# VectorE's operations inside each step of a 32-step lane chain, in another order

## The chip, the cores and the metric

The kernel runs on one core of a Trainium2 chip. Its time is the device time of one execution in microseconds (us). Three executions of the kernel before took 301.94, 303.7 and 392.66 us, median 303.7. A fourth was profiled: it took 303.54 us, and the span from its first to its last instruction is 301.7 us.

The engines are named as in the profile: PE is TensorE (PEld its weight loads), DVE is VectorE, ACT is ScalarE, POOL is GpSimd, SP is SyncE.

## What is computed

Two blocks of a network on 2048 tokens of width 128, all in fp32. The first block adds to x a recurrent memory and an expert network; the second adds attention and a gated network. The change lies in the recurrent memory alone:

```python
def step(M, kv):
    k_t, v_t = kv
    v_pred = jnp.einsum('bf,bfd->bd', k_t, M)
    surprise = jnp.linalg.norm(v_t - v_pred, axis=-1, keepdims=True)
    delta = k_t[:, :, None] * v_t[:, None, :]
    M = M + eta_c[None, :, None] * surprise[:, :, None] * delta
    return (_ln2(M), None)          # (M - mean) * rsqrt(var + eps), over all of M
M, _ = jax.lax.scan(step, M0, (kT, vT))     # 2048 tokens, one after the other
mem_out = jnp.einsum('btf,bfd->btd', q, M)
```

Only the last M is used. Each step needs one number of the step before, the surprise (a norm), and the spread of M (a variance).

## The kernel before

**The lanes.** The 2048 steps of the recurrence are cut into lanes of L = 32 tokens that overlap by half (HALF = 16), one lane for each of the 128 partitions. So 2048 dependent steps become 32 dependent steps (j = 0 to 31), each on 128 lanes at once. M itself is never formed: a lane keeps the inner products that the norm and the variance need, as short rows of numbers in the tiles ST (running rows), Y (weighted sums of products), Cr and CC (tables). All of them lie in one big tensor, so each reads `arena` in the profile.

**One step of the chain** is written out by hand, and every engine works its instructions off in the order in which they are written. In step j DVE does, by its lines in the kernel before:

- L1375, the scan: one `tensor_tensor_scan` of 17 elements, whose partial sums are what the step needs. It waits for ACT's result g of the step before, and for all that DVE wrote.
- L1382 and L1383, alpha and alpha2: two operations on one element each; the second reads the first. alpha2 releases ACT.
- L1391, the near product: adds a term to Y for the tokens of the same half (210 elements in steps 0 and 16, down to 2 in steps 13 and 29).
- L1397, the far product (steps 0 to 12, `FAR` = 13): 496 down to 304 elements, written to one of three buffers (`N_FP`), for PE, which adds it up in PSUM (L541). In steps 13 to 15 it is instead L1408, straight into Y.
- L1411, the row of squares (1 to 17 elements), and L1413, top (one element): both read Y, so they wait for the product before them.
- L1416, the rows: adds Cr, with the squares in it, to ST. The next scan reads ST.

Step 13 has three more: L1402 (GA), L1405 (GY, which reads what PE summed) and L1406 (a reduction of GY into ST).

**ACT** in step j: L917 (square root of the scan's last sum, after the scan), L919 (a copy), then L922, which waits for alpha2 and for L917 and gives g, the SG entry that scales everything in step j+1. Behind these it does other work in its queue where it falls due: L885 in steps 0 to 2, copies of PE's results (L897, L900 to L903, L907) after steps 5, 6, 7, 9, 10 and 11, and in step 13 the copy L933, for which DVE's L1405 waits. A copy that waits for PE holds up the L917 and L922 queued behind it.

**PE** adds up the far product of each step (L541), and after those of steps 4, 5, 6, 8, 9 and 10 does a piece of another job (L525 to L535), whose result ACT copies. After step 12 it goes on to the expert network (L554) and then has nothing until the chain has ended.

**Waiting inside an engine.** Two helpers order DVE's own work: `did(i)` lets instruction i raise a semaphore when it has finished, and `need(n)` lets the next instruction wait until the nth of these has finished; `last()` is `need` of the newest. An instruction with no such wait may start while the one before it is finishing.

**Behind the chain** come a few small operations, the memory's output (L560), the first block's sum, the second layer norm, and attention with the gated network, to the end.

The change touches the loop over j on DVE, L1360 to L1416.

Of the kernel before, what the change touches and what calls it, by code (L numbers as in the profile page):

```python
# [6 lines left out]
ALU = mybir.AluOpType  # L7
ACT = mybir.ActivationFunctionType
AX = mybir.AxisListType
# [8 lines left out]
HALF = 16  # L18
S = T // HALF
L = 2 * HALF  # L20
W = S
# [20 lines left out]
PAD = 30  # L42
RW = PAD + L + 4
R_G, R_T, R_Q, R_CD, R_D, R_C, R_R, R_B, R_S, R_P, R_E = 0, 1, 2, 5, 6, 9, 10, 13, 14, 15, 16
SCAN = R_E + 1
FAR = 13
FAR_BANK = 4
# [16 lines left out]
class Order:  # L64
# [5 lines left out]
    def did(self, instruction):  # L70
        instruction.then_inc(self.semaphore, 1)
        self.n += 1
        return self.n

    def need(self, n):
        self.engine.wait_ge(self.semaphore, n + self.offset)


def program(nc, a, out):
    with ExitStack() as ctx:  # L80
# [63 lines left out]
        CC = take(3 * (L + 1) * L).rearrange("p (q j t) -> p q j t", q=3, j=L + 1)  # L144
# [4 lines left out]
        Cr = Crf.rearrange("p (j r c) -> p j r c", j=L, r=4)  # L149
# [29 lines left out]
        def near(block, j):  # L179

            n = HALF - 2 - j
            return OJN[block][:, NEAR_AT[j]:NEAR_AT[j] + (n + 1) * n].rearrange("p (l t) -> p l t", t=n)
# [997 lines left out]
        def _(dve):  # L1180
            v = nc.vector
# [4 lines left out]
            def last():  # L1186
                need(o.n)
# [169 lines left out]
            dve.wait_ge(near_ready, 1)  # L1357
            last()

            for j in range(L):  # L1360
                sg = SG[:, j, 1:2]
                n = L - 2 - j
                end = HALF if j < FAR else L

                def of_scan(r):

                    c = PAD + j + 1 + 2 * (r - R_P)
                    return ST[:, R_P, c:c + 1]

                last()  # L1370
                dve.wait_ge(g_ready, j + 1)
                if j == HALF:
                    dve.wait_ge(behind_act, 9)
                c = PAD + j + 1 - 2 * R_P
                v.tensor_tensor_scan(ST[:, R_P, c:c + 2 * SCAN - 1:2], SG[:, j, :], ST[:, :, PAD + j], 0.0, ALU.mult, ALU.add).then_inc(scan_ready, 1)  # L1375
                if j == L - 1:
                    break

                dve.wait_ge(scan_ready, j + 1)
                if j == HALF - 1:  # L1380
                    dve.wait_ge(behind_act, 6)
                need(did(v.scalar_tensor_tensor(out=AL[:, j, 0:1], in0=of_scan(R_R), scalar=of_scan(R_R), in1=of_scan(R_Q), op0=ALU.mult, op1=ALU.add)))  # L1382
                v.scalar_tensor_tensor(out=AL[:, j, 1:2], in0=of_scan(R_E), scalar=VJ[:, j + 1:j + 2], in1=AL[:, j, 0:1], op0=ALU.mult, op1=ALU.add).then_inc(alpha_ready, 1)  # L1383

                jb = j % HALF
                nb = HALF - 2 - jb
                if nb > 0:

                    tail = (j // HALF + 1) * HALF
                    later = Y[:, j:tail - 1, j + 2:tail]  # L1390
                    did(v.scalar_tensor_tensor(out=later, in0=near(j // HALF, jb), scalar=sg, in1=later, op0=ALU.mult, op1=ALU.add))  # L1391
                if j < FAR:

                    if j >= N_FP:
                        dve.wait_ge(far_done, j - N_FP + 1)
                    vc_, a_ = far_factors(j)
                    v.scalar_tensor_tensor(out=FPf[j % N_FP][:, 0:(L - 1 - j) * HALF].rearrange("p (l t) -> p l t", t=HALF), in0=vc_, scalar=sg, in1=a_,  # L1397
                                           op0=ALU.mult, op1=ALU.mult).then_inc(fp_ready, 1)
                elif j < HALF:
                    if j == FAR:  # L1400

                        ga = did(v.tensor_tensor(GA, aT[:, 0:FAR, HALF:L], SG[:, 0:FAR, 1:2].broadcast_to([W, FAR, HALF]), ALU.mult))  # L1402
                        dve.wait_ge(far_act, 1)
                        need(ga)
                        need(did(v.tensor_tensor(GY, GA, PS[:, FAR_BANK, 0:FAR * HALF].rearrange("p (l t) -> p l t", t=HALF), ALU.mult)))  # L1405
                        did(v.tensor_reduce(ST[:, R_Q, PAD + HALF - 1:PAD + L - 1], GY.rearrange("p l t -> p t l"), AX.X, ALU.add))  # L1406
                    later = Y[:, j:L - 1, HALF:L]
                    did(v.scalar_tensor_tensor(out=later, in0=OJF[j - FAR], scalar=sg, in1=later, op0=ALU.mult, op1=ALU.add))  # L1408
                last()
                if end - j - 2 > 0:  # L1410
                    did(v.tensor_tensor(Cr[:, j, 0, j + 1:end - 1], CC[:, 0, j + 1, j + 2:end], Y[:, j, j + 2:end], ALU.mult))  # L1411
                if n > 0:
                    did(v.tensor_tensor(ST[:, R_T, PAD + j + 1:PAD + j + 2], CC[:, 0, j + 2, j + 2:j + 3], Y[:, j + 1, j + 2:j + 3], ALU.mult))  # L1413
                    need(o.n - 1)
                rows = ST[:, R_Q:R_S + 1:4, PAD + j + 1:PAD + L]
                did(v.scalar_tensor_tensor(out=rows, in0=Cr[:, j, :, j + 1:L], scalar=sg, in1=rows, op0=ALU.mult, op1=ALU.add))  # L1416


            dve.wait_ge(h_ready, L)
# [285 lines left out]
```

## Time and profile before

| what | value |
|---|---|
| median of three runs | 303.7 us |
| profiled execution | 303.54 us, its span 301.7 us |
| DVE, PE, ACT busy in the span | 236.7, 246.6, 189.0 us |
| first scan of the chain starts | 52.71 us |
| last scan starts | 106.18 us |
| the chain, from the one to the other | 53.47 us, 31 steps |

A row of a timeline gives an instruction's start and its duration. The distance between the starts of two neighbours is the number to watch in this case: it is sometimes shorter than the duration of the first of them, sometimes longer.

### The profile page before, as it was taken

Reading aid. Unit: us, or ns where it says so; the run is one execution under the profiler, and the core shown is the slowest. Engines: PE = TensorE matmul, PEld = TensorE weight load, DVE = VectorE, ACT = ScalarE, POOL = GpSimd, SP = SyncE. Lnnn points to the kernel's source line nnn. Section 1 sums busy time; section 2 is a strip of 40 time slices with the busy share of each in tenths; the row PEclk is TensorE's granted clock in tenths of the full one; section 3 lists DMA queues with packets and bytes.
Section 4 is the critical chain, followed back from the end, with each engine's and each line's share of the span. In section 5 each row is a group of like instructions: output and inputs, shape, how many; then the busy total and the mean of one; then the engine's idle time right before and its main releaser. Section 6 shows DMA issues by size and latency. Waiting matters only on the chain.

```text
span 301.7 us, 5258 instructions
## 1 busy us (share of the span) xinstructions
PE 246.6 (82%) x1730; PEld 166.5 (55%) x1730; DVE 236.7 (78%) x751; ACT 189.0 (63%) x452; POOL 99.2 (33%) x121
## 2 busy tenths in 40 slices
PE   0599978478830069997999999999998999999991
PEld 0339963133730066564678787777887444444481
DVE  6969789999899848985999997887775566666672
ACT  1249675646344413797787579999963877777630
POOL 8013000000000000789888546998895000000000
PEclk9999999999995555899999999999999999999999
DMA  7600000000000006400300000000000000000013
GB/s 204 184 6 4 2 0 0 3 1 0 0 3 0 1 1 239 180 0 12 130 1 3 0 2 1 0 2 1 2 0 2 0 0 3 0 0 0 3 35 109
DMA packets 8429, 8.57 MB, mean 28 GB/s; under 512 B 1744, under 2 KB 7504, under 8 KB 7888
## 3 DMA queue, kind: packets, MB, share of 16 engines
q1 hardware_dynamic: 7968, 7.91, 8.2%
q10 hardware_dynamic: 432, 0.30, 0.3%
q8 instruction: 16, 0.26, 0.3%
q14 instruction: 13, 0.11, 0.1%
HBM read 7.15 MB, written 1.05 MB: 27 GB/s over the span
## 4 chain that ended last, share of the span: by engine, by line
PE 57%; DVE 30%; ACT 7%; issue 3%; DMA 1%; SPq 0%; DVEq 0%; ACTq 0%
PE PS L749 9%; PE PS L750 9%; PE PS L707 9%; PE PS L687 8%; PE PS L698 4%; PE PS L452 3%; DVE arena L1416 3%; PE PS L467 2%; DVE arena L1382 2%; DVE arena L1397 2%; DVE arena L1383 2%; DVE arena L1375 2%; PE PS L560 2%; DVE arena L1391 2%; PE PS L664 2%
## 5 line engine op out<-in xcount | busy, mean ns | idle before, releaser
L749 PE MATMUL PS<-arena 128*128 128x512 f16 x128 | 48.5, 379 | 0.6 <-issue 0.6
L750 PE MATMUL PS<-arena 128*128 128x512 f16 x128 | 48.5, 379 | 0.0
L1633 DVE TENSOR_TENSOR arena<-arena 128x512 f32<-128x512 f32 x32 | 22.2, 692 | 19.5 <-ACT arena L1082 19.5
L687 PE MATMUL PS<-arena 128*128 128x512 f32 (+3 forms) x80 | 32.0, 531 | 0.4 <-ACT arena L1003 0.4
L1131 POOL CAST arena<-arena 128x512 f16<-128x512 f32 x2 | 1.2, 611 | 90.6 <-DVE x L1501 90.6
L1081 ACT ACTIVATE arena<-PS,arena 128x512 f32<-128x512 f32 x32 | 22.0, 688 | 13.2 <-PE PS L750 13.1
L1123 POOL TENSOR_TENSOR arena<-arena 128x256 f32<-128x256 f32 x32 | 21.6, 675 | 16.0 <-DVE arena L1572 13.7
L1055 ACT ACTIVATE arena<-PS,lnt 128x512 f32<-128x512 f32 (+3 forms) x40 | 25.0, 634 | 1.7 <-DVE lnt L1587 1.6
L1124 POOL TENSOR_TENSOR arena<-arena,small 128x256 f16<-128x256 f32 (+1 forms) x36 | 24.3, 676 | 2.8
L1580 DVE TENSOR_REDUCE mxb<-PS 128x1 f32<-128x512 f32 (+3 forms) x40 | 22.2, 602 | 1.8 <-PE PS L689 1.8
L1082 ACT ACTIVATE arena<-PS,arena 128x512 f16<-128x512 f32 x32 | 21.8, 682 | 0.0
L749 PEld LDWEIGHTS PS<-arena 128*128 128x128 f16 x128 | 12.5, 98 | 15.7 <-issue 0.7
L750 PEld LDWEIGHTS PS<-arena 128*128 128x128 f16 x128 | 12.5, 98 | 15.0
L687 PEld LDWEIGHTS PS<-arena 128*128 128x128 f32 x80 | 14.0, 190 | 12.2 <-issue 10.3
L698 PE MATMUL PS<-con,arena 128*128 128x128 f32 x136 | 19.6, 274 | 0.4 <-ACT arena L1055 0.4
L707 PE MATMUL PS<-arena,xn 128*128 128x128 f32 x144 | 19.3, 279 | 0.4 <-ACT xn L1039 0.2
L917 ACT ACTIVATE arena<-arena 128x1 f32<-128x1 f32 x32 | 6.5, 203 | 20.7 <-DVE arena L1375 20.6
L541 PE MATMUL PS<-arena,con 128*128 128x496 f32 (+12 forms) x26 | 12.2, 551 | 8.8 <-DVE arena L1397 7.3
L707 PEld LDWEIGHTS PS<-arena,xn 128*128 128x128 f32 x144 | 17.4, 191 | 1.5 <-ACT xn L1039 1.1
L568 PE MATMUL PS<-con,arena 128*32 128x1 f32 x2 | 0.3, 202 | 21.4 <-DVE arena L1422 21.4
L707 PE MATMUL PS<-arena 128*128 128x128 f32 x128 | 17.3, 279 | 0.3 <-ACT arena L1039 0.2
L698 PEld LDWEIGHTS PS<-con,arena 128*128 128x128 f32 x136 | 15.1, 141 | 3.6 <-issue 1.7
(263 smaller groups left out, 643.2 us busy)
## 6 DMA issues: line engine op xcount, KB each, us to landing
arena<-h_T SPq DMA_DIRECT2D x2, 1024.0 KB, 4.8
x<-L_attn_x SPq DMA_DIRECT2D x4, 256.0 KB, 4.6
arena<-cos SPq DMA_DIRECT2D x1, 1024.0 KB, 4.7
arena<-sin SPq DMA_DIRECT2D x1, 1024.0 KB, 6.9
out<-arena SPq DMA_DIRECT2D x4, 256.0 KB, 3.3
arena<-w_T SPq DMA_DIRECT2D x3, 256.0 KB, 3.0
con<-shape_constants ACTq DMA_DIRECT2D x1, 192.0 KB, 3.4
w1e<-L_ffn_W SPq DMA_DIRECT2D x1, 128.0 KB, 3.9
```

What stands on the lines that cost most here:

```text
L687: i = mm(PS[:, k, 0:cnt * P], qT1[:, t * P:(t + 1) * P], kT1[:, c * P:(c + cnt) * P], start=True, stop=not last)
L698: i = tr(PS[:, 4 + gi % 2, (b - c) * P:(b - c + 1) * P], Pr[t % 2][:, b * P:(b + 1) * P], ident)
L707: i = mm(PS[:, 7, (t % 4) * D:(t % 4 + 1) * D], PT[t % 2][:, b * P:(b + 1) * P], V1[:, b, :], start=(b == 0), stop=(b == t))
L749: mm(bank(u % 8), wH[:, k, m * P:(m + 1) * P], sH[:, k, cols], start=(k == 0), stop=False)
L750: i = mm(bank(u % 8), wL[:, k, m * P:(m + 1) * P], sL[:, k, cols], start=False, stop=(k == HT4 - 1))
L1055: f(Pr[t % 2][:, c * P:(c + cnt) * P], PS[:, SCORE_BANK[gi], 0:cnt * P], ACT.Exp, scale=1.0 / D, bias=nbs[:, t:t + 1], accum_out=rsums[:, ...
L1081: f(FP[u % 4], bank(u % 8), ACT.Gelu, scale=s_[:, u % HT4:u % HT4 + 1])
L1082: f(high, bank(u % 8), ACT.Gelu, scale=s_[:, u % HT4:u % HT4 + 1]).then_inc(read, 1)
L1123: o.need(o.did(tt(rest, value, high, ALU.subtract)))
L1124: return tt(low, rest, low_scale.broadcast_to([P, cols]), ALU.mult)
L1580: i = did(v.tensor_reduce(mxb[:, gi:gi + 1], PS[:, SCORE_BANK[gi], 0:cnt * P], AX.X, ALU.max))
L1633: v.tensor_tensor(RP[m], FP[m], high, ALU.subtract).then_inc(rest_ready, 1)
```

## The change

Inside each step DVE's operations stand in another order, and each waits for the one operation whose result it needs instead of for the newest. No operation is added or removed (711 instructions of DVE before and after), nothing changes in size, and the queues of the other engines stay as they are.

```diff
--- before.py
+++ after.py
@@ -1357,9 +1357,12 @@
             dve.wait_ge(near_ready, 1)
             last()
 
+            formed = added = o.n
             for j in range(L):
                 sg = SG[:, j, 1:2]
                 n = L - 2 - j
+                jb = j % HALF
+                nb = HALF - 2 - jb
                 end = HALF if j < FAR else L
 
                 def of_scan(r):
@@ -1367,7 +1370,7 @@
                     c = PAD + j + 1 + 2 * (r - R_P)
                     return ST[:, R_P, c:c + 1]
 
-                last()
+                need(max(formed, added))
                 dve.wait_ge(g_ready, j + 1)
                 if j == HALF:
                     dve.wait_ge(behind_act, 9)
@@ -1376,19 +1379,50 @@
                 if j == L - 1:
                     break
 
+                if nb > 0:
+
+                    tail = (j // HALF + 1) * HALF
+                    later = Y[:, j:tail - 1, j + 2:tail]
+                    added = did(v.scalar_tensor_tensor(out=later, in0=near(j // HALF, jb), scalar=sg, in1=later, op0=ALU.mult, op1=ALU.add))
+                if FAR < j < HALF:
+                    later = Y[:, j:L - 1, HALF:L]
+                    added = did(v.scalar_tensor_tensor(out=later, in0=OJF[j - FAR], scalar=sg, in1=later, op0=ALU.mult, op1=ALU.add))
+                if j == FAR:
+
+                    ga = did(v.tensor_tensor(GA, aT[:, 0:FAR, HALF:L], SG[:, 0:FAR, 1:2].broadcast_to([W, FAR, HALF]), ALU.mult))
+
                 dve.wait_ge(scan_ready, j + 1)
+                alpha = did(v.scalar_tensor_tensor(out=AL[:, j, 0:1], in0=of_scan(R_R), scalar=of_scan(R_R), in1=of_scan(R_Q), op0=ALU.mult, op1=ALU.add))
+
+                def row_of_squares():
+
+                    need(added)
+                    return did(v.tensor_tensor(Cr[:, j, 0, j + 1:end - 1], CC[:, 0, j + 1, j + 2:end], Y[:, j, j + 2:end], ALU.mult))
+
+                if end - j - 2 > 0 and j != FAR:
+                    formed = row_of_squares()
+
+                need(alpha)
                 if j == HALF - 1:
                     dve.wait_ge(behind_act, 6)
-                need(did(v.scalar_tensor_tensor(out=AL[:, j, 0:1], in0=of_scan(R_R), scalar=of_scan(R_R), in1=of_scan(R_Q), op0=ALU.mult, op1=ALU.add)))
                 v.scalar_tensor_tensor(out=AL[:, j, 1:2], in0=of_scan(R_E), scalar=VJ[:, j + 1:j + 2], in1=AL[:, j, 0:1], op0=ALU.mult, op1=ALU.add).then_inc(alpha_ready, 1)
 
-                jb = j % HALF
-                nb = HALF - 2 - jb
-                if nb > 0:
-
-                    tail = (j // HALF + 1) * HALF
-                    later = Y[:, j:tail - 1, j + 2:tail]
-                    did(v.scalar_tensor_tensor(out=later, in0=near(j // HALF, jb), scalar=sg, in1=later, op0=ALU.mult, op1=ALU.add))
+                if j == FAR:
+
+                    dve.wait_ge(far_act, 1)
+                    later = Y[:, j:L - 1, HALF:L]
+                    added = did(v.scalar_tensor_tensor(out=later, in0=OJF[j - FAR], scalar=sg, in1=later, op0=ALU.mult, op1=ALU.add))
+                    need(ga)
+                    gy = did(v.tensor_tensor(GY, GA, PS[:, FAR_BANK, 0:FAR * HALF].rearrange("p (l t) -> p l t", t=HALF), ALU.mult))
+                    formed = row_of_squares()
+                    need(gy)
+                    summed = did(v.tensor_reduce(ST[:, R_Q, PAD + HALF - 1:PAD + L - 1], GY.rearrange("p l t -> p t l"), AX.X, ALU.add))
+                if n > 0:
+                    need(added)
+                    top = did(v.tensor_tensor(ST[:, R_T, PAD + j + 1:PAD + j + 2], CC[:, 0, j + 2, j + 2:j + 3], Y[:, j + 1, j + 2:j + 3], ALU.mult))
+                need(summed if j == FAR else formed)
+                rows = ST[:, R_Q:R_S + 1:4, PAD + j + 1:PAD + L]
+                formed = did(v.scalar_tensor_tensor(out=rows, in0=Cr[:, j, :, j + 1:L], scalar=sg, in1=rows, op0=ALU.mult, op1=ALU.add))
                 if j < FAR:
 
                     if j >= N_FP:
@@ -1396,24 +1430,6 @@
                     vc_, a_ = far_factors(j)
                     v.scalar_tensor_tensor(out=FPf[j % N_FP][:, 0:(L - 1 - j) * HALF].rearrange("p (l t) -> p l t", t=HALF), in0=vc_, scalar=sg, in1=a_,
                                            op0=ALU.mult, op1=ALU.mult).then_inc(fp_ready, 1)
-                elif j < HALF:
-                    if j == FAR:
-
-                        ga = did(v.tensor_tensor(GA, aT[:, 0:FAR, HALF:L], SG[:, 0:FAR, 1:2].broadcast_to([W, FAR, HALF]), ALU.mult))
-                        dve.wait_ge(far_act, 1)
-                        need(ga)
-                        need(did(v.tensor_tensor(GY, GA, PS[:, FAR_BANK, 0:FAR * HALF].rearrange("p (l t) -> p l t", t=HALF), ALU.mult)))
-                        did(v.tensor_reduce(ST[:, R_Q, PAD + HALF - 1:PAD + L - 1], GY.rearrange("p l t -> p t l"), AX.X, ALU.add))
-                    later = Y[:, j:L - 1, HALF:L]
-                    did(v.scalar_tensor_tensor(out=later, in0=OJF[j - FAR], scalar=sg, in1=later, op0=ALU.mult, op1=ALU.add))
-                last()
-                if end - j - 2 > 0:
-                    did(v.tensor_tensor(Cr[:, j, 0, j + 1:end - 1], CC[:, 0, j + 1, j + 2:end], Y[:, j, j + 2:end], ALU.mult))
-                if n > 0:
-                    did(v.tensor_tensor(ST[:, R_T, PAD + j + 1:PAD + j + 2], CC[:, 0, j + 2, j + 2:j + 3], Y[:, j + 1, j + 2:j + 3], ALU.mult))
-                    need(o.n - 1)
-                rows = ST[:, R_Q:R_S + 1:4, PAD + j + 1:PAD + L]
-                did(v.scalar_tensor_tensor(out=rows, in0=Cr[:, j, :, j + 1:L], scalar=sg, in1=rows, op0=ALU.mult, op1=ALU.add))
 
 
             dve.wait_ge(h_ready, L)
```

In the order rows below, the line numbers are those of the kernel that is named. The names in all of them are `arena`, so operations are told by line and size; the scan is printed as a SCALAR_TENSOR_TENSOR of 128x17.

DVE, step 4 (a step with a far product; steps 0 to 12 are alike), before: scan, alpha, alpha2, near product, far product, squares, top, rows, next scan.

```order
L1375 SCALAR_TENSOR_TENSOR arena<-arena 128x17 [waits g_ready,dve_order]
L1382 SCALAR_TENSOR_TENSOR arena<-arena 128x1 [waits scan_ready]
L1383 SCALAR_TENSOR_TENSOR arena<-arena 128x1 [waits dve_order]
L1391 SCALAR_TENSOR_TENSOR arena<-arena 128x11x10
L1397 SCALAR_TENSOR_TENSOR arena<-arena 128x432 [waits far_done]
L1411 TENSOR_TENSOR arena<-arena 128x10 [waits dve_order]
L1413 TENSOR_TENSOR arena<-arena 128x1
L1416 SCALAR_TENSOR_TENSOR arena<-arena 128x4x27 [waits dve_order]
L1375 SCALAR_TENSOR_TENSOR arena<-arena 128x17 [waits g_ready,dve_order]
```

The same step in the changed kernel:

```order
L1378 SCALAR_TENSOR_TENSOR arena<-arena 128x17 [waits g_ready,dve_order]
L1386 SCALAR_TENSOR_TENSOR arena<-arena 128x11x10
L1395 SCALAR_TENSOR_TENSOR arena<-arena 128x1 [waits scan_ready]
L1400 TENSOR_TENSOR arena<-arena 128x10 [waits dve_order]
L1408 SCALAR_TENSOR_TENSOR arena<-arena 128x1 [waits dve_order]
L1422 TENSOR_TENSOR arena<-arena 128x1 [waits dve_order]
L1425 SCALAR_TENSOR_TENSOR arena<-arena 128x4x27 [waits dve_order]
L1431 SCALAR_TENSOR_TENSOR arena<-arena 128x432 [waits far_done]
L1378 SCALAR_TENSOR_TENSOR arena<-arena 128x17 [waits g_ready,dve_order]
```

The near product has moved ahead of alpha, the squares between alpha and alpha2, and the far product behind the rows, just ahead of the next scan. Alpha2, which releases ACT, now comes fifth instead of third.

DVE, step 16 (steps 16 to 29 are alike), before:

```order
L1375 SCALAR_TENSOR_TENSOR arena<-arena 128x17 [waits behind_act,g_ready,dve_order]
L1382 SCALAR_TENSOR_TENSOR arena<-arena 128x1 [waits scan_ready]
L1383 SCALAR_TENSOR_TENSOR arena<-arena 128x1 [waits dve_order]
L1391 SCALAR_TENSOR_TENSOR arena<-arena 128x15x14
L1411 TENSOR_TENSOR arena<-arena 128x14 [waits dve_order]
L1413 TENSOR_TENSOR arena<-arena 128x1
L1416 SCALAR_TENSOR_TENSOR arena<-arena 128x4x15 [waits dve_order]
```

And in the changed kernel:

```order
L1378 SCALAR_TENSOR_TENSOR arena<-arena 128x17 [waits behind_act,g_ready,dve_order]
L1386 SCALAR_TENSOR_TENSOR arena<-arena 128x15x14
L1395 SCALAR_TENSOR_TENSOR arena<-arena 128x1 [waits scan_ready]
L1400 TENSOR_TENSOR arena<-arena 128x14 [waits dve_order]
L1408 SCALAR_TENSOR_TENSOR arena<-arena 128x1 [waits dve_order]
L1422 TENSOR_TENSOR arena<-arena 128x1 [waits dve_order]
L1425 SCALAR_TENSOR_TENSOR arena<-arena 128x4x15 [waits dve_order]
```

Here too the near product and the squares now stand ahead of alpha2.

DVE, step 13 in the changed kernel, without its scan. Before, the order was alpha, alpha2, near product, GA, GY (waits for ACT's copy, `far_act`), reduction, far product, squares, top, rows.

```order
L1386 SCALAR_TENSOR_TENSOR arena<-arena 128x2
L1392 TENSOR_TENSOR arena<-arena 128x208
L1395 SCALAR_TENSOR_TENSOR arena<-arena 128x1 [waits scan_ready]
L1408 SCALAR_TENSOR_TENSOR arena<-arena 128x1 [waits dve_order]
L1414 SCALAR_TENSOR_TENSOR arena<-arena 128x18x16 [waits far_act]
L1416 TENSOR_TENSOR arena<-arena,PS 128x208 [waits dve_order]
L1400 TENSOR_TENSOR arena<-arena 128x17 [waits dve_order]
L1419 TENSOR_REDUCE arena<-arena 128x16 [waits dve_order]
L1422 TENSOR_TENSOR arena<-arena 128x1 [waits dve_order]
L1425 SCALAR_TENSOR_TENSOR arena<-arena 128x4x18 [waits dve_order]
```

GA stands ahead of alpha, and the far product (L1414) now also waits for ACT's copy and is the first behind it.

## Rows read from the trace of the kernel before

**Rows 1.** Stretches: length; busy us by engine (instructions), granted PE clock, DMA share, GB/s
```profile
52.70:78.00 25.30, 16.51 (x46) 6.98 (x45) 23.87 (x105) 13.62 (x52) 0.00 (x0) 1.00 0.00 1
...
84.73:106.40 21.67, 1.03 (x10) 0.84 (x8) 19.24 (x103) 10.39 (x45) 0.00 (x0) 0.60 0.00 1
```
**Rows 2.** Waits inside the chain: who waited for whom, us, times, longest
```profile
DVE arena L1375 <- ACT arena L922: 0.4, 1, 0.4
```
**Rows 3.** Timeline of DVE, step 4: start, duration, instruction
```profile
61.27 0.20 DVE L1375 TENSOR_TENSOR_SCAN arena<-arena 128x17 f32<-128x17 f32 x1
61.50 0.22 DVE L1382 SCALAR_TENSOR_TENSOR arena<-arena 128x1 f32<-128x1 f32 x1
61.76 0.22 DVE L1383 SCALAR_TENSOR_TENSOR arena<-arena 128x1 f32<-128x1 f32 x1
61.89 0.33 DVE L1391 SCALAR_TENSOR_TENSOR arena<-arena 128x110 f32<-128x110 f32 x1
62.14 0.66 DVE L1397 SCALAR_TENSOR_TENSOR arena<-arena 128x432 f32<-128x432 f32 x1
62.72 0.16 DVE L1411 TENSOR_TENSOR arena<-arena 128x10 f32<-128x10 f32 x1
62.80 0.15 DVE L1413 TENSOR_TENSOR arena<-arena 128x1 f32<-128x1 f32 x1
62.91 0.33 DVE L1416 SCALAR_TENSOR_TENSOR arena<-arena 128x108 f32<-128x108 f32 x1
63.28 0.19 DVE L1375 TENSOR_TENSOR_SCAN arena<-arena 128x17 f32<-128x17 f32 x1
```
**Rows 4.** Timeline of DVE and ACT, step 30, the last before the last scan
```profile
104.94 0.19 DVE L1375 TENSOR_TENSOR_SCAN arena<-arena 128x17 f32<-128x17 f32 x1
...
105.43 0.22 DVE L1383 SCALAR_TENSOR_TENSOR arena<-arena 128x1 f32<-128x1 f32 x1
...
105.68 0.40 ACT L922 ACTIVATE arena<-arena 128x12 f32<-128x12 f32 x1 [0.21 <-DVE arena L1383]
106.18 0.20 DVE L1375 TENSOR_TENSOR_SCAN arena<-arena 128x17 f32<-128x17 f32 x1 [0.39 <-ACT arena L922]
```
**Rows 5.** Timeline of DVE, step 16, and the start of step 29
```profile
84.73 0.20 DVE L1375 TENSOR_TENSOR_SCAN arena<-arena 128x17 f32<-128x17 f32 x1
...
85.35 0.43 DVE L1391 SCALAR_TENSOR_TENSOR arena<-arena 128x210 f32<-128x210 f32 x1
...
86.34 0.19 DVE L1375 TENSOR_TENSOR_SCAN arena<-arena 128x17 f32<-128x17 f32 x1
...
103.62 0.19 DVE L1375 TENSOR_TENSOR_SCAN arena<-arena 128x17 f32<-128x17 f32 x1
```
**Rows 6.** Timeline of PE, the far product of step 6
```profile
66.75 0.94 PE L541 MATMUL PS<-arena,con 128*128 128x400 f32 x2 [0.47 <-DVE arena L1397]
```
**Rows 7.** Timeline of ACT, first copy of that job and the L917 behind it
```profile
68.75 0.39 ACT L900 ACTIVATE arena<-PS 128x256 f32<-128x256 f32 x1 [0.44 <-PE PS L531]
...
69.29 0.20 ACT L917 ACTIVATE arena<-arena 128x1 f32<-128x1 f32 x1
```
**Rows 8.** Timeline of ACT and DVE, step 13, from its scan to the next
```profile
78.00 0.19 DVE L1375 TENSOR_TENSOR_SCAN arena<-arena 128x17 f32<-128x17 f32 x1
...
79.04 0.39 ACT L933 ACTIVATE arena<-PS 128x288 f32<-128x288 f32 x1
...
79.87 0.51 DVE L1406 TENSOR_REDUCE arena<-arena 128x16 f32<-128x208 f32 x1
80.29 0.51 DVE L1408 SCALAR_TENSOR_TENSOR arena<-arena 128x288 f32<-128x288 f32 x1
...
81.38 0.19 DVE L1375 TENSOR_TENSOR_SCAN arena<-arena 128x17 f32<-128x17 f32 x1
```
**Rows 9.** Timeline of PE behind the chain, two pairs of the same shape
```profile
118.15 2.07 PE L627 MATMUL PS<-xT,arena 128*128 128x512 f32 x2 [0.69 <-ACT xT L969]
...
124.21 1.02 PE L627 MATMUL PS<-xT,arena 128*128 128x512 f32 x2
```

More of the change, by code:

```diff
@@ L1377, in _ @@
                     break
-                dve.wait_ge(scan_ready, j + 1)
-                if j == HALF - 1:
-                    dve.wait_ge(behind_act, 6)
-                need(did(v.scalar_tensor_tensor(out=AL[:, j, 0:1], in0=of_scan(R_R), scalar=of_scan(R_R), in1=of_scan(R_Q), op0=ALU.mult, op1=ALU.add)))
-                v.scalar_tensor_tensor(out=AL[:, j, 1:2], in0=of_scan(R_E), scalar=VJ[:, j + 1:j + 2], in1=AL[:, j, 0:1], op0=ALU.mult, op1=ALU.add).then_inc(alpha_ready, 1)
-                jb = j % HALF
-                nb = HALF - 2 - jb
                 if nb > 0:
@@ new lines, in _ @@
+                if j == FAR:
+                    ga = did(v.tensor_tensor(GA, aT[:, 0:FAR, HALF:L], SG[:, 0:FAR, 1:2].broadcast_to([W, FAR, HALF]), ALU.mult))
+                dve.wait_ge(scan_ready, j + 1)
+                alpha = did(v.scalar_tensor_tensor(out=AL[:, j, 0:1], in0=of_scan(R_R), scalar=of_scan(R_R), in1=of_scan(R_Q), op0=ALU.mult, op1=ALU.add))
+                def row_of_squares():
+                    need(added)
+                    return did(v.tensor_tensor(Cr[:, j, 0, j + 1:end - 1], CC[:, 0, j + 1, j + 2:end], Y[:, j, j + 2:end], ALU.mult))
@@ new lines, in _ @@
+                if end - j - 2 > 0 and j != FAR:
+                    formed = row_of_squares()
+                need(alpha)
+                if j == HALF - 1:
+                    dve.wait_ge(behind_act, 6)
+                v.scalar_tensor_tensor(out=AL[:, j, 1:2], in0=of_scan(R_E), scalar=VJ[:, j + 1:j + 2], in1=AL[:, j, 0:1], op0=ALU.mult, op1=ALU.add).then_inc(alpha_ready, 1)
+                if j == FAR:
[7 more added lines that the diff above has]
+                    summed = did(v.tensor_reduce(ST[:, R_Q, PAD + HALF - 1:PAD + L - 1], GY.rearrange("p l t -> p t l"), AX.X, ALU.add))
```

## The prediction

> **What bounds the kernel now.** I read the stretches first, then the waits inside the chain, then the timeline of single steps, with start-to-start distances instead of durations. In the stretches [rows 1] the reader is to see that DVE is busy 23.87 of 25.30 us while the far products run and 19.24 of 21.67 us after them, where PE has 1.03 us of work; so the chain of 31 steps, 53.47 us, stands alone on the path, and whatever it gives up, the end should get. The waits say who limits it: DVE's scan waited for ACT once in 31 steps, for 0.4 us [rows 2]. So DVE's own sequence sets the step, and ACT's answer lies ready each time but the last.
>
> The timeline of step 4 shows where that sequence loses time [rows 3]. An operation that needs nothing of its neighbour starts before it ends: the near product 0.13 us behind alpha2 of 0.22 us, the far product 0.25 behind one of 0.33, the squares 0.58 behind 0.66, top 0.08 behind 0.16. The distance is the duration less 0.08 us. One that reads the result starts later than its end: alpha 0.23 behind a scan of 0.20, alpha2 0.26 behind 0.22, the rows 0.19 behind the start of the squares of 0.16, the next scan 0.37 behind rows of 0.33. There the distance is the duration plus 0.035 us. So each neighbourly dependence costs 0.115 us, and step 4 has four of them: 0.23 + 0.26 + 0.13 + 0.25 + 0.58 + 0.19 + 0.37 = 2.01 us.
>
> **Steps 0 to 12, with a far product.** I work out step 4 in the new order by the same two rules. Scan to near product 0.12; near product to alpha 0.25; alpha to alpha2 0.26, with the squares (0.08) inside that distance; alpha2 to top 0.14; top to rows 0.08, since the squares are long done; rows to far product 0.33 - 0.08 = 0.25; far product to the next scan 0.66 - 0.08 = 0.58, since the scan waits for the rows, which ended under it. Sum 1.68, against 2.01: 0.33 us saved, and with unrounded distances 0.34. No term of the saving depends on a size, so 13 steps give 13 x 0.34 = 4.4 us.
>
> ACT must keep up. From alpha's start to the next scan by way of alpha2 and ACT, step 30 shows the path bare [rows 4]: alpha started 0.23 behind the scan at 104.94, and the next scan came at 106.18, so 1.24 - 0.23 = 1.01 us. In step 4 alpha would start at 0.12 + 0.25 = 0.37, so ACT allows a step of 1.38, under 1.68. In steps 0 to 12 DVE stays the bound.
>
> The far product is later, though, and with it PE and ACT's copies of PE's other job. In step 6's case PE took the far product up at 66.75, as soon as it was there [rows 6], and ACT, held by four copies from 68.75, was free for L917 at 69.29 [rows 7]: 2.54 us after PE began. In the new order PE would begin 0.13 us behind the scan of step 7 (0.08 of the product are left then, and 0.05 to hand over), so ACT comes free 2.67 behind it. Step 8's scan stands 1.55 behind step 7's (the size falls with j), and its L917 wants to start 0.23 behind that, at 1.78. It starts 0.89 late; from L917 over L922 to the next scan are 0.20 + 0.03 and 0.50 us, so step 8 takes 2.67 - 1.55 + 0.73 = 1.85 us instead of 1.51. A stall of 0.35 us. The same collision comes a second time, in step 11, behind the two wide copies; I put it at 0.25 us by the same working. Steps 0 to 12 together: 4.4 - 0.6 = 3.8 us.
>
> **Step 13.** Its length is 3.38 us, and ACT's copy L933 starts 1.04 us behind the scan [rows 8]. The copy stands behind L922, and L922 behind alpha2, which now follows near product, GA and alpha: alpha starts at 0.12 + 0.14 + 0.29 = 0.55 (GA is 0.37 us long, as GY), alpha2 at 0.80, L922 at 1.05, the copy 0.31 later at 1.36, its end at 1.75. Behind it: far product 0.43, GY 0.37, reduction 0.51, rows 0.29, and three dependences, 0.035 each, with the squares beside them: scan at 3.48. This step loses 0.1 us.
>
> **Steps 14 and 15.** The product (0.49 us) now stands ahead of alpha, so alpha starts at 0.12 + 0.41 = 0.53 and ACT's path makes the step 0.53 + 1.01 = 1.54, against 1.68: together 0.3 us saved.
>
> **Steps 16 to 29.** DVE's own sum for step 16: 0.12 + 0.35 + 0.26 + 0.14 + 0.08 + 0.28 + 0.035 = 1.27 us. ACT's path: alpha starts at 0.12 + 0.35 = 0.47, and 0.47 + 1.01 = 1.48. ACT's is longer, so here the bound changes hands: not DVE but the loop over ACT sets the step. Step 16 took 1.61 [rows 5], so 0.13 is saved. In step 29 the product is down to 2 elements, about 0.22 us: 0.12 + 0.14 + 1.01 = 1.27 against 1.32 (103.62 to 104.94), 0.05 saved. Between these ends it falls evenly, and the mean of 0.10 over 14 steps gives 1.4 us. Step 30 has no product and stays.
>
> **Sum.** 3.8 - 0.1 + 0.3 + 1.4 = 5.4 us by hand; the same rules carried through all 31 steps with unrounded values, which give 53.67 us for the order before (0.2 more than the trace), give 47.90 for the new one, 5.8 less. I take 5.7. Against the profiled execution's 303.54 us that is 297.8; the median of the runs lies 0.2 above it, so I forecast **298.0 us**, 1.9% less, with a span of 296.0 and a chain of 47.8 us.
>
> **Unknown prices.** No row shows what follows a scan without a dependence. The bounds are 0.23 us start to start, as its dependent follower has it, and 0.12, as every other kind here allows (the reduction of 0.51 us is followed after 0.42 [rows 8]). I take 0.12, because two-input operations and a reduction agree on 0.08 to 0.09. At 0.23 the chain is 50.9 us and the saving 2.8. The new waits (top for the product, squares for the product) are met before their turn by 0.02 us in the case of the squares; if each cost 0.035, steps 0 to 15 would lose some 0.5 us. The clock behind the chain is the other unknown. The granted clock is 0.60 in the mean of the stretch in which PE idles [rows 1], and behind the chain a pair of 512-column products took 2.07 us at 118.15 and 1.02 at 124.21 [rows 9], 1.2 and 2.4 GHz. PE's pause, 21.67 less 1.03 us [rows 1], shrinks by only some 2 us, because its expert work starts sooner too, so it will be at 1.2 GHz again when the chain ends; where in that work it rises need not move along with the chain. Each us of dense work at the lower level costs half a us; 3 us earlier or later are 1.5 us either way at most, less where DVE is the slower.
>
> **A rule against this change.** The rows show overlap of independent neighbours by 0.08 us and a price of 0.035 for a wait [rows 3]. The Trainium skill, "VectorE: DVE Perf Modes", section "The DRAIN you can't avoid", says that the next op doesn't start until the pipe of the one before is empty, and that a semaphore between them costs nothing extra. By that rule the chain would come out as in the first rival below; the trace disagrees with it in each of the distances above.
>
> **Rivals.** *Operations follow end to start, and waits are free* (chance 4%). Then order gains nothing on DVE: in steps 0 to 12 the sum of durations is the same, and from step 13 on the near product and the squares in front of alpha2 delay ACT. In step 16, 0.20 + 0.43 + 0.22 + 0.17 put alpha2 at 1.02, and 0.22 + 0.03 + 0.50 behind it make 1.77 us, where DVE's sum is 1.67. Over steps 13 to 29 that is 1.9 us more than the same reckoning gives for the order before: 305.6. It decides if neighbours overlap by less than about 0.03 us where a wait is free. For it speaks only that no row shows the new neighbours. *The scan does not overlap* (14%): 2.8 saved, 300.9 us. *The stalls over PE and ACT are larger*, or waits that are met cost something (10%): another 0.8 us, 298.8. *The stalls don't come, or the clock rises sooner relative to the work* (12%): 1 to 1.5 us better, 296.7. *The clock rises later by many us* (4%): 12 us of dense work at 1.2 GHz would eat all of the gain, 304. The forecast as worked out keeps 56%.
>
> **Range and chances.** The middle case spans 296.9 to 299.2 by the clock; the range must take in the scan's bound, so 296.3 to 301.2, which leaves out the two slow cases and part of the best. A measurement of this kernel tells about 2% from no change, and 2% below 303.7 is 297.6, a little below my forecast. The middle case falls below it about one time in two and a half (0.24 of its 0.56), with the better case (0.12) and a little of the others: faster 0.39. Slower by over 2% needs over 309.8: 0.02. The rest, 0.59, is within 2%.
>
> **What would show it.** In the changed profile: near product 0.12 behind the scan; step 4 at 1.68 us; steps 16 to 29 with DVE idle ahead of the scan, waiting for ACT's L922, about 0.2 us each time, where only one such wait stood before; steps 8 and 11 longer than their neighbours by 0.35 and 0.25, with the scan waiting for ACT; step 13 at 3.5; the last scan some 5.7 us sooner, and the same distance at the end of the span. I am wrong if alpha starts more than 0.4 us behind the scan in step 4, or if the chain gets its 5.7 us and the span does not.

## The result, and the profile after

The changed kernel took 298.0 us, the median of four runs (297.84 to 298.56), against 303.6 us of the kernel before: a ratio of 0.984, 95% interval 0.980 to 0.987. The ratio leaves out the one slow run of the kernel before, 392.66 us. The profiled execution took 298.56 us with a span of 296.8. The forecast was 298.0 us with a span of 296.0.

First the waits. The next view lists, of the waits inside the chain, those of DVE (us in all, times, longest); before, the scan waited for ACT once [rows 2].

```profile
DVE arena L1378 <- ACT arena L922: 5.5, 18, 0.4
DVE arena L1414 <- ACT arena L933: 0.8, 1, 0.8
DVE arena L1378 <- DVE arena L1425: 0.3, 1, 0.3
```

L1378 is the scan in the changed kernel. It now waits for ACT 18 times, 5.5 us in all: behind steps 8 and 11, and behind 16 of the 17 steps from 14 on. DVE is less busy than it was, although it does the same operations: in the stretch of steps 16 to 30, 15.10 of 19.81 us, where it had been 19.24 of 21.67 [rows 1]. Time in which two operations overlap counts once.

```profile
82.06:101.87 19.81, 1.82 (x17) 1.63 (x15) 15.10 (x102) 10.38 (x45) 0.00 (x0) 0.63 0.00 1
```

Step 4 on DVE's timeline (start, duration, instruction) answers to [rows 3]. L1386 is the near product, L1395 and L1408 alpha and alpha2, L1400 the squares, L1422 top, L1425 the rows, L1431 the far product.

```profile
61.43 0.20 DVE L1378 TENSOR_TENSOR_SCAN arena<-arena 128x17 f32<-128x17 f32 x1
61.54 0.32 DVE L1386 SCALAR_TENSOR_TENSOR arena<-arena 128x110 f32<-128x110 f32 x1
61.78 0.21 DVE L1395 SCALAR_TENSOR_TENSOR arena<-arena 128x1 f32<-128x1 f32 x1
61.91 0.16 DVE L1400 TENSOR_TENSOR arena<-arena 128x10 f32<-128x10 f32 x1
62.03 0.22 DVE L1408 SCALAR_TENSOR_TENSOR arena<-arena 128x1 f32<-128x1 f32 x1
62.16 0.15 DVE L1422 TENSOR_TENSOR arena<-arena 128x1 f32<-128x1 f32 x1
62.23 0.32 DVE L1425 SCALAR_TENSOR_TENSOR arena<-arena 128x108 f32<-128x108 f32 x1
62.48 0.66 DVE L1431 SCALAR_TENSOR_TENSOR arena<-arena 128x432 f32<-128x432 f32 x1
63.05 0.18 DVE L1378 TENSOR_TENSOR_SCAN arena<-arena 128x17 f32<-128x17 f32 x1
```

Each distance is shorter than the duration of the operation ahead; alpha to alpha2 still takes 0.25 us, but the squares lie in it. The durations are those of before; 1.62 us instead of 2.01 come from the distances. The near product stands 0.11 behind the scan: the price that no row of before showed.

A late step shows the loop over ACT. DVE and ACT, step 28:

```profile
98.10 0.20 DVE L1378 TENSOR_TENSOR_SCAN arena<-arena 128x17 f32<-128x17 f32 x1 [0.32 <-ACT arena L922]
98.21 0.21 DVE L1386 SCALAR_TENSOR_TENSOR arena<-arena 128x6 f32<-128x6 f32 x1
...
98.34 0.21 DVE L1395 SCALAR_TENSOR_TENSOR arena<-arena 128x1 f32<-128x1 f32 x1
...
98.59 0.22 DVE L1408 SCALAR_TENSOR_TENSOR arena<-arena 128x1 f32<-128x1 f32 x1
98.73 0.15 DVE L1422 TENSOR_TENSOR arena<-arena 128x1 f32<-128x1 f32 x1
98.80 0.22 DVE L1425 SCALAR_TENSOR_TENSOR arena<-arena 128x12 f32<-128x12 f32 x1
98.84 0.40 ACT L922 ACTIVATE arena<-arena 128x12 f32<-128x12 f32 x1 [0.22 <-DVE arena L1408]
99.34 0.19 DVE L1378 TENSOR_TENSOR_SCAN arena<-arena 128x17 f32<-128x17 f32 x1 [0.32 <-ACT arena L922]
```

DVE's rows end at 99.02; the next scan comes at 99.34, 0.10 behind the end of ACT's L922.

Where the time went, from the starts of the scans in both traces:

| part of the span | before | after | difference | forecast |
|---|---|---|---|---|
| up to the first scan | 52.71 | 54.44 | +1.73 | 0 |
| steps 0 to 12 | 25.29 | 21.16 | -4.13 | -3.8 |
| step 13 | 3.38 | 3.44 | +0.06 | +0.1 |
| steps 14 and 15 | 3.35 | 3.02 | -0.33 | -0.3 |
| steps 16 to 29 | 20.21 | 18.58 | -1.63 | -1.4 |
| step 30 | 1.24 | 1.23 | -0.01 | 0 |
| last scan to the end | 195.52 | 194.93 | -0.59 | 0 |
| span | 301.7 | 296.8 | -4.9 | -5.7 |

The column of the forecast has the hand-worked terms, which come to 5.4; the total is the 5.7 taken. The chain gave 6.04 us. The first line is not the change's: nothing was changed there. The same twelve matrix products ahead of the chain (L426) took 2.02 us in the trace of before and 3.81 in that of after:

```profile
15.39 2.02 PE L426 MATMUL PS<-arena,wkT 128*64 128x512 f32 x12 [0.42 <-DVE arena L1222]
```

```profile
15.33 3.81 PE L426 MATMUL PS<-arena,wkT 128*64 128x512 f32 x12 [0.27 <-DVE arena L1222]
```

In the ten profiled executions of this study they took anything from 2.02 to 3.81 us, and the first scan started between 52.6 and 54.5 us accordingly. So two single executions can differ by almost 2 us ahead of the chain, and the chain has to be compared by itself. That the median is 298.0 to the tenth is luck in part: the chain gave 0.3 us more than forecast, and the rest of the execution varies by more than that.

### The profile page after: what moved, and what is told of

The parts are those of the page before. It is cut to its first block, busy times and chain, and to the rows that moved or that the text cites. A ratio compares the mean times of both kernels' runs of the same rounds, so it can differ in the third digit from the quotient of the medians.

```text
span 296.8 us, 5257 instructions
## 1 busy us (share of the span) xinstructions
PE 247.8 (83%) x1730; PEld 166.7 (56%) x1730; DVE 228.4 (77%) x751; ACT 188.6 (64%) x452; POOL 99.2 (33%) x121
## 4 chain that ended last, share of the span: by engine, by line
PE 59%; DVE 24%; ACT 10%; issue 3%; DMA 1%; DVEq 0%; SPq 0%; ACTq 0%
PE PS L749 9%; PE PS L750 9%; PE PS L707 9%; PE PS L687 8%; PE PS L698 4%; PE PS L452 3%; ACT arena L922 3%; PE PS L467 2%; PE PS L560 2%; DVE arena L1378 2%; DVE arena L1386 2%; PE PS L664 2%; PE PS L665 2%; DVE arena L1408 2%; DMA x<-L_attn_x 1%
## 5 line engine op out<-in xcount | busy, mean ns | idle before, releaser
L922 ACT ACTIVATE arena<-arena 128x12 f32<-128x12 f32 x31 | 12.3, 397 | 8.9 <-DVE arena L1408 8.9
L1580 DVE SCALAR_TENSOR_TENSOR arena<-arena,PS 128x256 f32<-128x256 f32 x32 | 13.4, 420 | 4.3 <-ACT arena L1012 3.6
```

## The experiments

All of them start from the changed kernel, except the second. In each the chain's length is read from the scans' starts in the profiled execution, and the time is the median with its ratio to the kernel before on the same chip.

**Every operation waits for its neighbour.** The order stays; each of the loop's operations waits for the newest one.

```diff
-                need(max(formed, added))
+                last()
...
+                    dve.wait_ge(scan_ready, j + 1)     # the near product
...
+                last()                                 # alpha
                 dve.wait_ge(scan_ready, j + 1)
...
-                    need(added)                        # the squares
+                    last()
...
-                need(alpha)
+                last()
...
-                    need(added)                        # top
+                    last()
+                    dve.wait_ge(alpha_ready, j + 1)
...
-                need(summed if j == FAR else formed)
+                last()
...
+                    last()                             # the far product
                     vc_, a_ = far_factors(j)
```

> The order of the change is kept, but every operation of the chain's loop on DVE waits for the one just ahead of it (the scan alone does not wait for the far product). Theory A (a neighbour without a wait starts 0.08 us before the end, one with a wait 0.035 after it, so the gain of the change is in the waits and not in the order as such): step 4 becomes 0.23 + 0.355 + 0.245 + 0.195 + 0.255 + 0.185 + 0.355 + 0.58 = 2.40 us instead of 1.62, steps 16 to 29 grow by 0.42 us each (ACT's path), the chain by 15 to 17 us, from 47.4 to about 64; time about 314. Theory B (operations drain anyway and a semaphore costs nothing): chain and time stay, 47.4 and 298 us.

Measured: 317.06 us in one run, chain 68.36 us, 20.9 more than the changed kernel's. Step 4 took 2.59 us instead of 1.62, with the same durations (near product L1387, alpha L1399, squares L1404, alpha2 L1412, top L1428, rows L1431, far product L1438):

```profile
63.97 0.19 DVE L1378 TENSOR_TENSOR_SCAN arena<-arena 128x17 f32<-128x17 f32 x1
64.19 0.33 DVE L1387 SCALAR_TENSOR_TENSOR arena<-arena 128x110 f32<-128x110 f32 x1
64.56 0.22 DVE L1399 SCALAR_TENSOR_TENSOR arena<-arena 128x1 f32<-128x1 f32 x1
64.81 0.17 DVE L1404 TENSOR_TENSOR arena<-arena 128x10 f32<-128x10 f32 x1
65.02 0.22 DVE L1412 SCALAR_TENSOR_TENSOR arena<-arena 128x1 f32<-128x1 f32 x1
65.34 0.16 DVE L1428 TENSOR_TENSOR arena<-arena 128x1 f32<-128x1 f32 x1
65.54 0.33 DVE L1431 SCALAR_TENSOR_TENSOR arena<-arena 128x108 f32<-128x108 f32 x1
65.97 0.67 DVE L1438 SCALAR_TENSOR_TENSOR arena<-arena 128x432 f32<-128x432 f32 x1
```

Theory B is out: with every operation waiting for its neighbour, the new order is 13.5 us slower than the kernel before. The dependences are the cost. The sum fell short by 4 us, though. Most distances are the duration plus 0.035, as reckoned, but alpha2 to top is 0.32 and rows to far product 0.43, each 0.10 behind the end. These two are the operations with two waits, and the one written last is the open one. The far product shows it within this run: up to step 2 it has only the one wait, and there it starts 0.04 behind the rows. Step 0:

```profile
54.95 0.35 DVE L1431 SCALAR_TENSOR_TENSOR arena<-arena 128x124 f32<-128x124 f32 x1
...
55.34 0.73 DVE L1438 SCALAR_TENSOR_TENSOR arena<-arena 128x496 f32<-128x496 f32 x1
```

I came back to that in the experiment on the scan's two waits. At 0.065 us for each of 29 tops and of 10 far products it makes some 2.5 of the 20.9 us (an estimate). The rest of the miss lies mostly in steps 16 to 29, which grew by 0.52 us each and not by 0.42: where I had reckoned with ACT's path, the scan followed DVE's own rows, by 0.03 us. In this run PE also stood at a granted clock of 0.50 from 61 to 71 us; the scan followed DVE's operations there all the same, the steps being 2.5 us long.

**The far product last, and nothing else**, on the kernel before: the block of L1392 to L1398 moves behind L1416.

```diff
-                if j < FAR:
-                    ...                                # the far product, as it is
-                elif j < HALF:
+                if FAR <= j < HALF:
...
                 did(v.scalar_tensor_tensor(out=rows, in0=Cr[:, j, :, j + 1:L], scalar=sg, ...))
+                if j < FAR:
+                    ...                                # the far product, as it is
```

> The order before, with one move alone: the far product of steps 0 to 12 goes behind the rows. Theory A: in the old order the far product already stood between the near product and the squares that wait for it; behind the rows it covers the scan's wait for the rows instead, and uncovers the squares' wait. One dependence is traded for another: chain 53.5 us, time 303.6, no difference. ACT's late copies find room in steps of 1.9 us and cost nothing. Rival: moving the far product last is what brings the gain of steps 0 to 12; then 0.115 us for each of 13 steps at least, 1.5 us: chain 52, time 302.1.

Measured: 303.5 us in ten runs against 303.55, ratio 1.0, interval 0.997 to 1.003. Steps 0 to 5 and 9 to 30 are as long as before to 0.02 us, but for step 3, 0.06 shorter. Moved alone, the far product trades one bare dependence for another and brings nothing; the gain of steps 0 to 12 needs other moves with it. Which of the others it needs, the near product's or the squares', was not tried one by one. The profiled execution had a chain of 54.6 us, 1.1 longer, and all of it in steps 6 to 8: 2.87 instead of 1.92 us, then 2.03 and 1.94. The stretch shows why (PE busy is the first number behind the length, the granted clock the third from the right):

```profile
62.00:68.00 6.00, 5.39 (x8) 2.32 (x8) 4.89 (x22) 2.09 (x8) 0.00 (x0) 0.50 0.00 0
```

PE stood at 1.2 GHz there, its pair for a far product of 416 columns took 1.59 us instead of 0.97, and ACT waited for PE (2.45 us ahead of a copy, L897) with the scan's root behind it. In the trace of before the clock in these six us is 1.00. So the hand-over to PE has a second price, which falls due when PE's clock drops while the far products run. It did in two of ten profiled executions, this one and the first experiment's; there the longer steps hid it. Whether the old order would have stalled at that clock too, no run shows.

**The far product in the middle.** The same block of the changed kernel, back behind alpha2.

```diff
+                if j < FAR:
+                    ...                                # the far product, as it is
                 if j == FAR:
                     dve.wait_ge(far_act, 1)
...
                 formed = did(v.scalar_tensor_tensor(out=rows, ...))
-                if j < FAR:
-                    ...
```

> The changed kernel with the far product of steps 0 to 12 back behind alpha2, ahead of top. Theory A: the scan waits for the rows bare again, 0.115 us in each of 13 steps, 1.5 us; but PE gets the product 0.5 us sooner, so steps 8 and 11 lose their waits for ACT (some 0.35 us each): chain 47.4 + 1.5 - 0.7 = 48.2, time 298.8. Rival (the long steps 8 and 11 do not come from the far product's place): they stay at 1.84 + 0.1 and 1.78 + 0.1 us, chain 48.9, time 299.5.

Measured: 298.81 us, ratio 0.985 (0.980 to 0.989), chain 48.08 us. Steps 0 to 7, 9, 10 and 12 are longer by 0.12 us, two of them by less (step 3 by 0.07, step 6 by 0.01, where the changed kernel lost some time to ACT too): the scan's wait for the rows, laid bare. Step 0 takes 1.93 us here, against 2.20 in the kernel before and 1.81 in the changed one: with the near product and the squares moved, 0.27 us is gained with the far product in the middle, and another 0.12 with it last, the same move that alone brought nothing. Steps 8 and 11 took 1.60 and 1.50, down from 1.84 and 1.78: no stall. Both halves of theory A hold, to 0.1 us.

**ACT's copies one step later.**

```diff
-                for k in BEHIND_AT.get(j - 1, ()):
+                for k in BEHIND_AT.get(j - 2, ()):
                     behind(k)
```

> The changed kernel with ACT's copies of PE's other job one step later each (behind steps 6, 7, 8, 10, 11 and 12 instead of 5, 6, 7, 9, 10 and 11). Theory A: ACT no longer stands waiting for PE with the next step's L917 and L922 behind it, so steps 8 and 11 come down from 1.84 and 1.78 to about 1.50 and 1.40 us, no other step grows: chain 46.7, time 297.3. Rival (it is the copies' own length on ACT, not the wait for PE, that delays L917): the long steps only move on by one, to 9 and 12, chain 47.4, time 298.0.

Measured: 295.92 us, ratio 0.974 (0.969 to 0.979), chain 46.54, 0.89 us shorter. Steps 8 and 11 took 1.46 and 1.37, step 6 came down from 1.65 to 1.54, and no other step grew by more than 0.02. In the changed kernel ACT's copies and the L917 behind them look so in step 8:

```profile
68.31 0.39 ACT L900 ACTIVATE arena<-PS 128x256 f32<-128x256 f32 x1 [0.83 <-PE PS L531]
...
68.82 0.22 ACT L917 ACTIVATE arena<-arena 128x1 f32<-128x1 f32 x1
...
69.14 0.40 ACT L922 ACTIVATE arena<-arena 128x12 f32<-128x12 f32 x1
...
69.63 0.19 DVE L1378 TENSOR_TENSOR_SCAN arena<-arena 128x17 f32<-128x17 f32 x1 [0.30 <-ACT arena L922]
```

And with the copies one step later:

```profile
68.30 0.40 ACT L922 ACTIVATE arena<-arena 128x12 f32<-128x12 f32 x1 [0.26 <-DVE arena L1408]
68.60 0.36 ACT L900 ACTIVATE arena<-PS 128x256 f32<-128x256 f32 x1
...
69.21 0.20 ACT L917 ACTIVATE arena<-arena 128x1 f32<-128x1 f32 x1
```

In the changed kernel ACT sat 0.83 us ahead of L900 waiting for PE, and L917 came right behind the copies. With the copies one step later the result is there, and the same copies fit between two steps. The wait was the cost, not the copies. The time fell by 2.1 us, more than the chain, and the expectation (297.3) was missed by 1.4: the rest of the execution was shorter as well (193.8 us behind the last scan instead of 194.9), which the edit does not touch.

**The product cut in two** from step 14 on.

```diff
-                need(max(formed, added))
+                need(formed)
...
+                    if j > FAR:
+                        if tail - 1 - j > 2:
+                            second = later[:, 2:, :], factor[:, 2:, :]
+                        later, factor = later[:, 0:2, :], factor[:, 0:2, :]
+                    need(rest)
                     added = did(v.scalar_tensor_tensor(out=later, in0=factor, scalar=sg, in1=later, ...))
...
+                if second:                             # behind the rows
+                    rest = did(v.scalar_tensor_tensor(out=second[0], in0=second[1], scalar=sg, in1=second[0], ...))
```

> The changed kernel with the product ahead of alpha cut in two from step 14 on: the two rows of Y that this step still needs (at most 32 elements) stay ahead of alpha, the rest goes behind the rows, where DVE waits for ACT anyway; the next product, not the scan, waits for it. Theory A (from step 14 on the loop over ACT sets the step, and it is lengthened by all of the product that stands ahead of alpha): steps 16 to 29 come down from 1.46 to 1.24 to an even 1.30 to 1.24 us, 1.1 us in all, and steps 14 and 15 by some 0.15 us each; chain 47.4 to 46.1, time 296.6. Rival (DVE's own sum sets the step): the same elements in two operations cost 0.14 us more in each step, chain 49.3, time 299.8.

Measured: chain 46.09 us as expected, 297.05 us, ratio 0.977 (0.972 to 0.983). Steps 16 to 29 took 1.24 to 1.30 us, flat, where they had fallen from 1.46 to 1.24 with the product's size; steps 14 and 15 took 1.30 each. DVE does one more operation in each of steps 14 to 28, and the steps are shorter. So from step 14 on the bound is the loop scan, alpha, alpha2, ACT, scan, and what stands ahead of alpha counts.

**The scan's two waits in the other order.**

```diff
-                need(max(formed, added))
                 dve.wait_ge(g_ready, j + 1)
+                need(max(formed, added))
```

> The changed kernel with the two waits ahead of the scan in the other order: first for ACT's g, then for DVE's own rows. In all runs so far the scan starts 0.10 us behind the end of ACT's L922 where it waits for that, but 0.04 behind the rows where it waits for those. Theory A (of two waits the one written last costs 0.065 us more if it is the open one): the scan starts 0.035 behind L922 from step 14 on, 17 steps, 1.0 us: chain 46.4, time 297.0. Theory B (0.10 us is what a hand-over from ACT to DVE costs): no step changes, 47.4 and 298.0.

Measured: 296.06 us, ratio 0.976 (0.970 to 0.981), chain 46.14, 1.29 us shorter. ACT's g and the scan, steps 16 and 17:

```profile
82.72 0.40 ACT L922 ACTIVATE arena<-arena 128x12 f32<-128x12 f32 x1 [0.43 <-DVE arena L1408]
83.15 0.19 DVE L1378 TENSOR_TENSOR_SCAN arena<-arena 128x17 f32<-128x17 f32 x1 [0.20 <-ACT arena L922]
```

The scan starts 0.03 behind the end of L922, where it had been 0.10. Steps 14 to 30 are shorter by 0.06 to 0.12 us each, 1.2 us together; the rest came from steps 3, 6 and 11, in which ACT was late too. And step 13, in which the open wait is the one for DVE's own rows, went from 3.44 to 3.52: the price went over to it. Theory A holds in both directions, and it fits the 0.10 us of the first experiment, where the far product changed from 0.04 to 0.10 as its second wait came in. What it is in the engine that costs this, I haven't shown.

**The copy first in step 13.** The block of L933 moves ahead of L922 in ACT's loop.

```diff
+                    if j == FAR:
+                        act.wait_ge(far_done, FAR)
+                        f(Y[:, FAR:L - 1, HALF:L], PS[:, FAR_BANK, ...], ACT.Copy).then_inc(far_act, 1)
                     act.wait_ge(alpha_ready, j + 1)
```

> The changed kernel with ACT's copy of PE's sum (L933) ahead of L922 in step 13. Theory A (the 0.1 us that step 13 lost comes from that copy standing behind L922, and L922 behind alpha2): the copy starts as soon as PE is done, some 0.4 us sooner, and step 13 comes down from 3.44 to about 3.05 us; g is not needed before that. Rival (the copy waits for PE): step 13 stays at 3.44.

Measured: step 13 took 3.11 us, 0.33 less (expected 0.4), chain 47.11; one run of 298.78 us, too coarse to show it. The copy stands under L922 here, being ahead of L925, which gives g:

```profile
75.83 0.78 PE L541 MATMUL PS<-arena,con 128*128 128x304 f32 x2 [0.94 <-DVE arena L1431]
...
76.65 0.41 ACT L922 ACTIVATE arena<-PS 128x288 f32<-128x288 f32 x1 [0.44 <-PE PS L541]
...
77.10 0.52 DVE L1414 SCALAR_TENSOR_TENSOR arena<-arena 128x288 f32<-128x288 f32 x1 [0.42 <-ACT arena L922]
```

It now waits for PE's last sum, which ends at 76.61; that is the next bound of this step, and it comes from the far product of step 12 being last.

**All four edits together**: the later copies, the copy first, the cut product, the swapped waits.

> Four edits on the changed kernel together: ACT's copies one step later, L933 ahead of L922 in step 13, the product cut in two from step 14 on, the scan's waits in the other order. Theory A: 0.9 + 0.4 + 1.3 + 0.95 us (the last a little less, as DVE's own sum is close behind in the first steps after 16): chain 47.4 to 43.9, time 294.4. Rival (the steps behind 16 are already as short as DVE's own sum allows once the product is cut): the fourth edit adds nothing, chain 44.9, time 295.4.

Measured: 294.05 us in six runs, ratio to the kernel before 0.969 (0.965 to 0.974), chain 43.86 us against 43.9 expected. This version beats both kernels (the changed one has a ratio of 0.984, 0.980 to 0.987, on its own chip): the chain is 9.6 us shorter than before, and 3.6 shorter than with the change alone. Step 18 of it (DVE and ACT; here L1393 and L1431 are the two parts of the product, L1412 is alpha2 and L925 gives g) comes to 1.2 us:

```profile
81.87 0.19 DVE L1378 TENSOR_TENSOR_SCAN arena<-arena 128x17 f32<-128x17 f32 x1
81.99 0.24 DVE L1393 SCALAR_TENSOR_TENSOR arena<-arena 128x24 f32<-128x24 f32 x1
...
82.15 0.21 DVE L1399 SCALAR_TENSOR_TENSOR arena<-arena 128x1 f32<-128x1 f32 x1
...
82.40 0.22 DVE L1412 SCALAR_TENSOR_TENSOR arena<-arena 128x1 f32<-128x1 f32 x1
...
82.66 0.40 ACT L925 ACTIVATE arena<-arena 128x12 f32<-128x12 f32 x1 [0.26 <-DVE arena L1412]
82.79 0.35 DVE L1431 SCALAR_TENSOR_TENSOR arena<-arena 128x132 f32<-128x132 f32 x1
```

DVE is busy again up to the scan: the rest of the product fills the time in which it used to wait.

## Why the prediction was right

- **What bounds the chain.** Right. What left the chain left the time: against the kernel before, 6.0 us of chain went with 5.6 us of time in the changed kernel, 9.6 with 10 in the last version, and 14.9 us more chain went with 13.5 more in the first experiment. What else differed between the two profiled executions (+1.73 ahead, -0.59 behind) lies in stretches that no edit touches, and it varies by as much between the executions of the experiments (193.7 to 196.0 us behind the last scan). What varies behind the chain is not shown.
- **Steps 0 to 12: 0.34 us from each.** Right in kind, a little low: steps with no stall gave 0.38 to 0.40. In step 4 six of the seven distances came out 0.01 us shorter than worked out (the scan is followed after 0.11 us instead of 0.12, the rows stand 0.07 behind top instead of 0.08, and so on): the two rules hold. The first experiment shows that the gain is in the waits; the second, that the far product's move alone does not bring it.
- **The stalls of steps 8 and 11.** Right in place and mechanism, as the third and fourth experiments show from two sides. The one in step 8 was reckoned as 1.85 us and measured as 1.84. The one in step 11 was put at 0.25 "by the same working" without rows for it and came to about 0.4. Step 6 lost 0.1 too, which the forecast had left out.
- **Step 13: 0.1 lost.** Measured 0.06, and moving the copy ahead of L922 took 0.33 us off this step, which is the stated reason. The terms of the forecast add up to 3.46 us, not to the 3.48 written there; 3.44 was measured.
- **Steps 14 to 29: the bound changes hands.** Right. The scan waits for ACT, as foretold, for about 0.3 us each time where I had said 0.2. Step 16 took 1.46 (1.48 forecast), step 29 1.30 (1.27). The 1.4 us in between were reckoned with a mean of 0.10, where the two ends give 0.09 and 1.3 us; measured are 1.63, because the saving did not fall evenly: it was still 0.10 to 0.14 us in steps 18 to 28 and 0.02 in step 29. In step 29 L922 starts 0.09 behind alpha2 instead of 0.03; why is not shown. The cut product shows it is the loop over ACT. Inside that loop I took 0.10 us from ACT's end to the scan from [rows 4] as given; two thirds of it were the order of two waits.
- **The scan's overlap** was the open price with the largest stake, 3 us. It lies at the cheap end, 0.11 us. It had been chosen by analogy, and the trace bears it out.
- **The rule against the change.** The forecast gave only half of what the Trainium skill, "VectorE: DVE Perf Modes", section "The DRAIN you can't avoid", says. The section lets the pipe run empty between operations, but adds: "A next op that is not held starts earlier". With that the trace agrees: an operation with no wait on its neighbour starts 0.08 us before that one's end. The section also says, of eight copies in a row, that the semaphore costs nothing extra. By that the first experiment should have changed nothing, and here the trace disagrees: 20.9 us.
- **The chances.** I had put 0.39 on more than 2% faster and 0.59 on within 2%; at 1.6% the latter came. What the sum couldn't tell is the part of the time outside the chain, which varies by 2 us ahead of it and by as much behind.

## What to carry to other kernels

Where an engine works through short dependent operations, read start-to-start distances, not durations: here each dependence between neighbours costs 0.115 us more than independent neighbours do, half as much as a one-element operation, and an independent one put in between fills that time. Shortening one engine's part of a loop can hand the bound to the loop over the next engine. Here, what stood ahead of the operation that releases that engine then counted in full, and what stood behind it was free as long as it fitted into the wait. If an operation of DVE has two waits, write the one that is open longest first.

## What the runs showed of the hardware that I had not expected

- With two waits ahead of an operation on DVE, the start came 0.10 us behind the event when the open wait was the one written last, and 0.03 to 0.04 when it was written first or was the only one. In step 13, DVE's L1414 starts 0.03 behind the end of ACT's L933 with one wait (changed kernel), and the same operation (L1419 there) 0.10 behind it with a second wait written ahead (first experiment). Swapping the scan's two waits took 1.29 us off a chain of 31 steps.
- A stretch in which PE is part idle may or may not lose its clock. Between 62 and 68 us, with PE doing one far product in each step of 2 us, the granted clock was 1.00 in the trace of before and 0.50 in that of the far product last, at much the same load ahead of it (PE busy 2.97 and 3.19 of the 6 us from 55 to 61, clock 1.00 in both). The changed kernel was busy for the same 3.19 us there and kept its clock.
- The twelve products of L426 took 2.02 to 3.81 us in different executions, while the view gives a granted clock of 1.00 for all of them. The stored record of the clock begins with an entry of 1.00, at different times: about 14.0 us of the span in the trace of before and in that of the far product last, 16.6 in the first experiment, 17.0 to 17.1 in three others, and 18.8 to 19.1 in four, the changed kernel's among them. The products start at 15.2 to 15.4 us and took 2.02, 2.59, 2.79 to 2.83, and 3.76 to 3.81 us, in this order of the executions. Half rate up to that entry would make them 2.02, 2.6, 2.8 to 2.9, and 3.8 to 3.9 (an estimate). So a later rise of PE's clock fits the 1.73 us that the changed kernel's execution lost ahead of the chain; what sets the moment of the rise is not shown.
